# Issue order of the token load and the zero fill at the start of a decoder kernel

## The chip, the core and the metric

The kernel runs on one core of one Trainium2 chip. The time is the device time of one execution in microseconds (us), given as the median of three runs. Besides it there is one profiled execution, whose span runs from the first to the last instruction.

The core has a matrix engine (PE), a vector engine (DVE), an activation engine (ACT), a general one (POOL), and SP, which here does nothing but issue the direct transfers. All of SP's transfers go into one queue that 16 DMA engines serve.

## The reference, cut to what matters

```python
x = x + _L0_attn_ref(_layernorm(x), ...)              # 16 heads, rotary positions
x = x + _L0_xattn_ref(_layernorm(x), itok, ctx, ctx, ctx)  # 4 experts, chosen by token id
x = x + _L0_ffn_ref(_layernorm(x), ...)               # two linears with sign weights
x = x + _L1_attn_ref(_layernorm(x), ...)
x = x + _L1_xattn_ref(_layernorm(x), ctx, mask, ...)
x = x + _L1_ffn_ref(_layernorm(x), ...)
```

`x` is 4 batches of 512 tokens of 512 numbers in float32 (4 MiB). The expert stage takes each token through the one expert that its id picks.

## The kernel before

The whole of `x` stays on the chip in the tile `x`, as 16 tiles of 128 tokens. Seven phases run one after the other with a barrier of all engines between them: `Start`, `Attention` (attn0), `Experts`, `BitMlp`, `Attention` twice more (attn1, xattn) and `Fp8Linear`. Only the first two are touched.

**Start** loads the constants and the tokens, normalises batch 0 into `xn`, and works out on DVE to which row of a sorted list each token belongs (`place`). The sorted list, `sorted_x`, is a tensor in DRAM of 19 slots of 128 rows; each expert's part is padded up to whole slots. So that the padding holds zeros, all of `sorted_x` is first filled from `zero`, the last 512 columns of `arena` (L263, semaphore `filled`, of which the later phase knows `m.zero_filled`). `x` is loaded in two pieces (L259): batch 0 with the semaphore `x_loaded[0]`, then batches 1 to 3 with `x_loaded[1]`, known later as `m.x_all`. Between the two, `sp_following` issues the first two weight matrices of attn0 (keys and queries).

**attn0** begins on SP with seven loads of constants (L552: biases, `rope_cos`, `rope_sin`, `rope_rot`), then `weights.sp_rest`: the value weights and the output weights (L356), each as soon as the buffer it reuses has been split into its two float16 halves (ACT L372, then DVE L376; `weight_low` counts those). Then SP waits for the constants and enters a loop over the batches. In it, SP issues 48 small copies (L568) that stack the projected keys and queries into `kst` and `qst`; the first 12 wait for two finished projections (`fl`, counted by POOL at L1064), the next 12 for four, then six, then eight. Behind them come the copies of the row maxima (L573).

The projections of one batch go so: PE makes projection `n` (12 matmuls, L389), ACT reads it with its bias into `qb` (L790), POOL multiplies by the cosines (L1025, `t1`), PE turns it by a matmul with `rot` (L651), DVE multiplies by the sines (L926), adds both (L930) and rounds (L932), POOL takes the low half (L1064). `qb` and `t1` have two buffers: ACT may read projection `n` only when `t1` of `n - 1` is there, so with no work from POOL two projections are read and no third. Then PE makes the values, mixed with the row maxima's matmuls (L599), of which the first waits for the first 24 stacking copies (`stacked[0]`).

POOL's part of attn0 (the function `pool`) begins with a memset (L1010), waits for the constants, and then, before it enters the loop over the batches, for the zero fill:

```python
if self.rope:
    g.wait_ge(*m.zero_filled)
with g.Fori(0, NB) as b:
```

This is there since POOL scatters the tokens into `sorted_x` at the end of every batch. `m.x_all` is waited for later: by POOL behind the projections of a batch, by DVE at its fourth unit of the heads.

Of the kernel before, what the change touches and what calls it, by code (L numbers as in the profile page):

```python
# [12 lines left out]
P = 128  # L13
NB = 4
# [4 lines left out]
T = S // P  # L19
# [30 lines left out]
class Chain:  # L50


    def __init__(self, phase, sem, per, b):
        self.at, self.sem, self.per, self.base, self.n = phase.at, sem, per, b * per, 0
# [12 lines left out]
class Machine:  # L67
# [53 lines left out]
    def take(self, n, dt=F32):  # L121

        words = (n + 1) // 2 if dt == F16 else n
        a = self.arena[:, self.used:self.used + words]
        self.used += words
        assert self.used <= ARENA, self.used
        return a if dt == F32 else a.bitcast(dt)
# [70 lines left out]
class Phase:  # L198
# [16 lines left out]
    def sp_following(self, sp):  # L215
        if self.following:
            self.following.sp_early(sp)

    def sp_early(self, sp): pass
# [5 lines left out]
    def sp(self, sp): pass  # L225


class Start(Phase):
# [7 lines left out]
    def __init__(self, m):  # L236
        super().__init__(m, "start")
        s, take = self.sem, m.take
        self.x_loaded, self.const = self.sems("x_loaded", 2, 16), s("const_loaded", 16 * 4)
        self.norm = Norm(m, "norm", 1)  # L240
        self.consts, self.memsets, self.filled = s("consts_done", 2), s("ones_and_zero", 2), s("zero_filled", 16)
        n = NE * NB * T
        e_t = lambda a: a.rearrange("p (e t) -> p e t", e=NE)
        self.ids = take(NB * T, I32)
        self.own, self.total, self.before, self.rank = (e_t(take(n)) for _ in range(4))
        self.tri, self.ones, self.starts = take(P), take(P), take(NSLOT)
        self.cut = e_t(take(n))
        self.n, self.tiles, self.base = take(NE), take(NE), take(NE)
        self.placef, self.expertf = take(NB * T), take(NSLOT)
        self.zero = m.arena[:, ARENA - D:]  # L250
        self.own_made, self.counted, self.chain = s("experts_known", 1), s("tokens_counted", 1), s("chain", 60)
        m.zero_filled, m.x_all = self.at(self.filled, 16), self.at(self.x_loaded[1], 16)

    def sp(self, sp):
        m, io = self.m, self.io
        for dst, src in ((self.ids, io["itok_cols"]), (m.ident[:], io["ident"]), (self.tri, io["triangle"]), (self.starts, io["slot_starts"])):
            sp.dma_start(dst, src).then_inc(self.const, 16)
        for k, b in ((0, slice(0, 1)), (1, slice(1, NB))):
            sp.dma_start(m.x[:, b.start * T:b.stop * T, :], io["x"][b].rearrange("b (t p) d -> p (b t) d", p=P)).then_inc(self.x_loaded[k], 16)  # L259
            if k == 0:  # L260
                self.sp_following(sp)
        sp.wait_ge(*self.at(self.memsets, 2))
        sp.dma_start(io["sorted_x"].rearrange("(s p) d -> p s d", p=P),  # L263
                     self.zero.rearrange("p (a d) -> p a d", a=1).broadcast_to([P, NSLOT, D])).then_inc(self.filled, 16)

    def pool(self, g):
# [127 lines left out]
class Attention(Phase):  # L394
# [118 lines left out]
    def row(self, g, j):  # L513
        n = self.ROWS * g + j
        return n % 2, n // 2
# [23 lines left out]
    def sp(self, sp):  # L539
        m, io = self.m, self.io  # L540
        row = lambda a: a.rearrange("(a n) -> a n", a=1).broadcast_to([P, D])
        loads = [(self.vb, row(self.v_bias)), (self.ob, row(self.out_bias)),
                 (self.pb[:, 0:C], self.biases[0]),
                 (self.pb[:, C:2 * C], self.biases[1])]
        if self.rope:
            loads += [(self.cos, io["rope_cos"]), (self.sin, io["rope_sin"]), (self.rot, io["rope_rot"])]
        if self.cross:
            loads += [(self.gamma, row(io["L1_xattn_ln_gamma"])), (self.beta, row(io["L1_xattn_ln_beta"])),
                      (self.rs, io["L1_xattn_residual_scale"].rearrange("(a n) -> a n", a=1).broadcast_to([P, 1])),
                      (self.mask, io["mask_cols"])]  # L550
        for dst, src in loads:
            sp.dma_start(dst, src).then_inc(self.const, 16)  # L552
        self.weights.sp_rest(sp)
        sp.wait_ge(*self.at(self.const, 16 * len(loads)))

        with sp.Fori(0, NB) as b:
            if self.cross:
                nb = (b + 1) % NB
                sp.wait_ge(*self.at(self.audio_low, b + 1))
                sp.dma_start(m.raw[:, 0],  # L560
                             io["ctxT"][bass.ds(nb * D, D), :].rearrange("(c p) o -> p c o", p=P)).then_inc(self.audio_loaded, 16)
            for half in range(2):
                order = ((0, self.kst, (0, 0, 1)), (1, self.qst, (0, 1, 0)))
                for n, (w, stack, parts) in enumerate(reversed(order) if self.cross else order):
                    sp.wait_ge(*self.at(self.fl, b * self.NPROJ + 4 * half + 2 * (n + 1)))
                    for r, part in enumerate(parts):
                        for j in range(HG):
                            sp.dma_start(stack[HD * r:HD * (r + 1)].rearrange("p (c j) t -> p c j t", j=HG)[:, 2 * half:2 * half + 2, j, :],  # L568
                                         self.qf[HD * j:HD * (j + 1), w, part, 2 * half:2 * half + 2]).then_inc(self.stacked[half], 16)
            if not self.cross:  # L570
                for g in range(C):
                    self.row_wait(sp, self.row_free, self.row(g, self.ROWS - 1), b, 1)
                    sp.dma_start(self.qst[3 * HD:3 * HD + 1, HG * g:HG * (g + 1), :].rearrange("p h t -> p (h t)"),  # L573
                                 self.mt[0:HG * T, :]).then_inc(self.mdma, 16)
        if self.cross:
            sp.wait_ge(*self.at(self.audio_low, NB + 1))
        else:
            self.weights.wait(sp, len(self.weights.mats) - 1)
        if self.rope:
            for k in range(2):  # L580
                sp.wait_ge(*self.at(self.row_free[k], T // 2 + NB * (self.row_items // 2)))
        self.sp_following(sp)
        if self.rope:
            self.following.weights.sp_rest(sp)
# [1258 lines left out]
```

## Time and profile before

| | us |
|---|---|
| median of 3 runs | 2064.85 |
| lowest, highest | 2061.89, 2064.95 |
| span of the profiled execution | 2056.5 |
| median less this span | 8.35 |

The profiled execution has no time of its own beside its span; the 8.35 us between the span and the median are taken as what lies around it. The page of the profile gives shares of busy time over the whole span; for a change in the first 100 us of 2056.5 us, the list of instructions in order of time is of more use. In it, a bracket behind a row tells how long the engine was idle ahead of the row and what released it, and rows with SPq are transfers as SP issues them: their duration is that of the issue, not of the transfer.

### The profile page before, as it was taken

The numbers are of one execution on the slowest core, as the hardware profiler recorded it, in microseconds if no ns is written. First come the engines' busy times: TensorE is split into PE (matmuls) and PEld (weight loads), VectorE is DVE, ScalarE is ACT, GpSimd is POOL, SyncE is SP. The second block draws the span as 40 slices with busy tenths as digits, with TensorE's granted clock in tenths as the row PEclk, the third lists the DMA queues.
The fourth block names the chain that finished last, engine by engine and source line by source line (L and its number), as shares of the span: only waits on it lengthen the run. The fifth ranks groups of instructions, "written<-read, shape, count | busy, mean of one in ns | idle before, by whom it ended". The sixth has DMA issues, their size and how long they took to land.

```text
span 2056.5 us, 28429 instructions
## 1 busy us (share of the span) xinstructions
PE 1639.2 (80%) x9252; PEld 640.5 (31%) x9253; DVE 1369.1 (67%) x2092; ACT 854.3 (42%) x1015; POOL 522.9 (25%) x413
## 2 busy tenths in 40 slices
PE   1998898988948935777699899999697887877837
PEld 1323233232336622333323333232232312222213
DVE  3876867858645537999285564738547677666868
ACT  1152240532523315776435353534546262542613
POOL 1514216133120015111401212130232311313117
PEclk9999999999979977998899999999899999898968
DMA  7201103002124444000210202020330110202102
GB/s 284 63 2 36 46 0 80 2 22 60 42 91 143 143 128 62 1 0 0 80 34 3 60 0 61 0 51 10 123 82 21 33 28 20 61 20 51 31 5 82
DMA packets 80843, 106.08 MB, mean 52 GB/s; under 512 B 14112, under 2 KB 51360, under 8 KB 80672
## 3 DMA queue, kind: packets, MB, share of 16 engines
q1 hardware_dynamic: 77216, 97.14, 15.9%
q0 software_dynamic: 3584, 8.39, 2.0%
q8 instruction: 24, 0.39, 0.1%
q14 instruction: 19, 0.16, 0.0%
HBM read 49.26 MB, written 18.35 MB: 33 GB/s over the span
## 4 chain that ended last, share of the span: by engine, by line
PE 35%; issue 25%; DVE 19%; POOL 6%; SPq 5%; ACT 4%; DMA 3%; DVEq 1%; POOLq 0%; ACTq 0%
PE ps L389 13%; PE ps L630 11%; SPq L568 5%; DVE arena L825 5%; PE ps L599 5%; PE ps L729 4%; DVE arena L970 2%; DVE arena L845 2%; POOL arena L1064 2%; DVE stats L171 1%; ACT arena L806 1%; DVE arena L1486 1%; DMA arena<-arena 1%; DVE arena L1497 1%; PE ps L615 1%
## 5 line engine op out<-in xcount | busy, mean ns | idle before, releaser
L630 PE MATMUL ps<-arena 128*32 128x512 f32 x3072 | 399.5, 623 | 45.1 <-ACT arena L806 33.0
L825 DVE TENSOR_REDUCE arena<-ps 128x1 f32<-128x512 f32 x512 | 323.1, 678 | 147.3 <-PE ps L599 146.9
L806 ACT ACTIVATE arena<-ps 128x1024 f32<-128x1024 f32 x256 | 252.1, 1025 | 314.9 <-PE ps L729 313.8
L389 PE MATMUL ps<-xt,w 128*128 128x512 f16 (+1 forms) x1872 | 293.4, 310 | 36.1 <-DVE arena L876 17.9
L729 PE MATMUL ps<-arena 97*128 97x512 f16 (+1 forms) x768 | 216.8, 386 | 19.2 <-DVE arena L970 15.1
L599 PE MATMUL ps<-arena 96*128 96x512 f16 x512 | 186.8, 398 | 53.1 <-DMA arena<-arena 33.9
L389 PEld LDWEIGHTS ps<-xt,w 128*128 128x128 f16 (+1 forms) x1872 | 156.9, 100 | 176.3 <-issue 66.2
L389 PE MATMUL ps<-w,arena 128*128 128x512 f16 (+1 forms) x804 | 180.0, 381 | 12.7 <-issue 12.7
L806 ACT ACTIVATE arena<-arena 128x1024 f32<-128x1024 f32 x128 | 134.0, 1056 | 130.9 <-DVE arena L970 125.1
L970 DVE TENSOR_SCALAR arena<-ps,arena 128x1024 f32<-128x1024 f32 x128 | 157.1, 1256 | 38.4 <-PE ps L729 38.1
L1004 POOL TENSOR_TENSOR arena<-arena 128x512 f32<-128x512 f32 x36 | 57.2, 1589 | 447.3 <-DVE arena L845 447.3
L790 ACT ACTIVATE arena<-ps,arena 128x512 f32<-128x512 f32 x96 | 65.8, 686 | 250.8 <-PE ps L389 127.0
L630 PEld LDWEIGHTS ps<-arena 128*32 128x32 f32 x3072 | 78.1, 111 | 218.5 <-issue 187.4
L1064 POOL TENSOR_TENSOR arena<-arena 128x512 f16<-128x512 f32 x96 | 111.6, 1163 | 133.8 <-ACT arena L794 112.9
L845 DVE RECIPROCAL arena<-arena 128x128 f32<-128x128 f32 x144 | 132.4, 933 | 0.0
L599 PEld LDWEIGHTS ps<-arena 96*128 96x128 f16 x512 | 45.2, 98 | 250.9 <-DVE arena L825 178.4
L192 POOL TENSOR_TENSOR rstd<-mv,eps 128x4 f32<-128x4 f32 x30 | 6.5, 215 | 451.3 <-DVE mv L175 451.3
L838 DVE TENSOR_TENSOR xt<-ps,xt 128x512 f16<-128x512 f32 x60 | 40.6, 682 | 115.2 <-ACT xt L744 115.2
L389 PEld LDWEIGHTS ps<-w,arena 128*128 128x128 f16 x804 | 77.9, 98 | 114.6 <-issue 23.5
L389 PE MATMUL ps<-w,xt 128*128 128x512 f16 x384 | 111.1, 408 | 0.0
L729 PEld LDWEIGHTS ps<-arena 97*128 97x128 f16 (+1 forms) x768 | 68.5, 99 | 129.0 <-issue 51.1
L171 DVE BATCH_NORM_STATS2 stats<-x 128x6 f32 (+1 forms) x104 | 64.2, 680 | 22.4 <-DMA x<-sorted_y,place 16.7
(171 smaller groups left out, 2089.0 us busy)
## 6 DMA issues: line engine op xcount, KB each, us to landing
arena<-arena SPq DMA_DIRECT2D x576, 64.0 KB, 2.0
raw<-in_ctxT SPq DMA_DIRECT2D x8, 1024.0 KB, 5.4
raw<-in_ffn_parts SPq DMA_DIRECT2D x16, 512.0 KB, 3.5
sorted_x<-arena SPq DMA_DIRECT2D x1, 4864.0 KB, 29.4
arena<-sorted_x SPq DMA_DIRECT2D x19, 256.0 KB, 3.5
sorted_y<-arena SPq DMA_DIRECT2D x19, 256.0 KB, 2.1
out<-x SPq DMA_DIRECT2D x16, 256.0 KB, 2.1
x<-in_x SPq DMA_DIRECT2D x1, 3072.0 KB, 17.4
```

Source lines behind the costliest of these rows:

```text
L171: v.bn_stats(m.stats[:, i, :], src(i)).then_inc(self.sums, 1)
L389: last = pe.matmul(out, left[l](cl[k]), right[r](cr[k]), start=start and k == 0 and a == 0, stop=stop and k == n - 1 and a == 2)
L568: sp.dma_start(stack[HD * r:HD * (r + 1)].rearrange("p (c j) t -> p c j t", j=HG)[:, 2 * half:2 * half + 2, j, :], self.qf[HD * j:HD * (j ...
L599: pe.matmul(self.row_bank(at), self.qst[0:3 * HD, head, t * P:(t + 1) * P], self.kst[0:3 * HD, head, :], start=True, stop=True).then_inc(s ...
L630: last = pe.matmul(self.m.ps[HD * j:HD * (j + 1), 7 if ones else 6, :], left, self.pt[:, u % 2, j * S:(j + 1) * S], start=kb == 0, stop=kb ...
L729: last = pe.matmul(self.m.ps[:, j4, :], self.kst[0:R, HG * g + j4, kb * P:(kb + 1) * P], self.qst[0:R, HG * g + j4, :], start=True, stop=True)
L790: act.activation(self.qb[:, n % 2, :], self.bank(item), ACT.Identity, scale=s, bias=self.pb[:, C * w + c:C * w + c + 1]).then_inc(self.ban ...
L806: act.activation(out, src, ACT.Exp, scale=SOFTMAX_SCALE).then_inc(self.exp_done[h], 1)
L825: v.tensor_reduce(self.mx[:, j:j + 1], self.row_bank(at), AX.X, ALU.max).then_inc(self.row_free[at[0]], 1)
L845: v.reciprocal(part, part).then_inc(self.inverted, 1)
L970: v.tensor_scalar(self.pt[:, u % 2, 2 * h * S:(2 * h + 2) * S], flat(m.ps[:, 2 * h:2 * h + 2, :]), slot_col(self.hi, b * T + kb), -50.0 / ...
L1064: g.tensor_tensor(self.qf[:, w, 1, c, :], src[:, n % 2, :], self.qf[:, w, 0, c, :], ALU.subtract).then_inc(self.fl, 1)
```

## The change

The load of batches 1 to 3 and the zero fill are taken out of `Start.sp` and put into a function `sp_late`, which attn0 calls on SP behind its constants and the rest of its weights, ahead of the wait for the constants. The wait on the memsets ahead of the fill goes, since a barrier now lies between. No other engine's program changes; POOL still waits for the zero fill ahead of its loop.

```diff
         m.zero_filled, m.x_all = self.at(self.filled, 16), self.at(self.x_loaded[1], 16)
+        m.start_late = self.sp_late
...
-        for k, b in ((0, slice(0, 1)), (1, slice(1, NB))):
-            sp.dma_start(m.x[:, b.start * T:b.stop * T, :], io["x"][b].rearrange("b (t p) d -> p (b t) d", p=P)).then_inc(self.x_loaded[k], 16)
-            if k == 0:
-                self.sp_following(sp)
-        sp.wait_ge(*self.at(self.memsets, 2))
-        sp.dma_start(io["sorted_x"].rearrange("(s p) d -> p s d", p=P),
+        self.load_x(sp, slice(0, 1), self.x_loaded[0])
+        self.sp_following(sp)
+
+    def load_x(self, sp, b, loaded):
+        sp.dma_start(self.m.x[:, b.start * T:b.stop * T, :], self.io["x"][b].rearrange("b (t p) d -> p (b t) d", p=P)).then_inc(loaded, 16)
+
+    def sp_late(self, sp):
+
+        self.load_x(sp, slice(1, NB), self.x_loaded[1])
+        sp.dma_start(self.io["sorted_x"].rearrange("(s p) d -> p s d", p=P),
                      self.zero.rearrange("p (a d) -> p a d", a=1).broadcast_to([P, NSLOT, D])).then_inc(self.filled, 16)
...
         self.weights.sp_rest(sp)
+        if self.rope:
+            m.start_late(sp)
         sp.wait_ge(*self.at(self.const, 16 * len(loads)))
```

SP's queue before, from the query weights of attn0 on (the end of `Start` and the head of attn0; `in_L_attn_v_wT` are the value weights, `in_L_attn_out_wT` the output weights, `phase_end` is the barrier):

```order
L356 DMA raw<-in_L_attn_q_wT 128x4x512
L259 DMA x<-in_x 128x12x512
L263 DMA sorted_x<-arena 128x19x512 [waits ones_and_zero]
L552 DMA arena<-in_L_attn_v_b 128x512 [waits phase_end]
L552 DMA arena<-in_L_attn_out_b 128x512
L552 DMA arena<-in_L_attn_k_b_cols 128x4
L552 DMA arena<-in_L_attn_q_b_cols 128x4
L552 DMA arena<-in_rope_cos 128x512
L552 DMA arena<-in_rope_sin 128x512
L552 DMA arena<-in_rope_rot 128x128
L356 DMA raw<-in_L_attn_v_wT 128x4x512 [waits weight_low]
L356 DMA raw<-in_L_attn_out_wT 128x4x512 [waits weight_low]
```

The same place in the changed kernel, whose line numbers are up to 7 higher:

```order
L361 DMA raw<-in_L_attn_q_wT 128x4x512
L557 DMA arena<-in_L_attn_v_b 128x512 [waits phase_end]
L557 DMA arena<-in_L_attn_out_b 128x512
L557 DMA arena<-in_L_attn_k_b_cols 128x4
L557 DMA arena<-in_L_attn_q_b_cols 128x4
L557 DMA arena<-in_rope_cos 128x512
L557 DMA arena<-in_rope_sin 128x512
L557 DMA arena<-in_rope_rot 128x128
L361 DMA raw<-in_L_attn_v_wT 128x4x512 [waits weight_low]
L361 DMA raw<-in_L_attn_out_wT 128x4x512 [waits weight_low]
L263 DMA x<-in_x 128x12x512
L268 DMA sorted_x<-arena 128x19x512
```

The two large transfers have moved behind nine others, and behind the two waits on `weight_low`.

POOL in the changed kernel, at the head of attn0 (a memset, the branch into the loop with its waits, the first products with the cosines):

```order
L1017 MEMSET arena 1x8192 [waits phase_end]
L1024 UNCONDITIONAL_BRANCH [waits zero_filled,consts_done,const_loaded]
L1024 ISA
L503 ISA [waits norm_xn_ready]
L1031 ISA [waits bank_free0]
L1032 TENSOR_TENSOR arena<-arena 128x512 [waits rotated]
L1032 TENSOR_TENSOR arena<-arena 128x512 [waits rotated,bank_free1]
```

Nothing moved here: these rows stand in the same order before, with line numbers lower by 7.

## Rows read from the trace of the kernel before

**Rows 1.** The page: the chain that ended last, share of the span by engine.
```profile
PE 35%; issue 25%; DVE 19%; POOL 6%; SPq 5%; ACT 4%; DMA 3%; DVEq 1%; POOLq 0%; ACTq 0%
```

**Rows 2.** Timeline of SP: start, us, what it issues, count.
```profile
12.59 0.51 SPq L356 DMA_DIRECT2D raw<-in_L_attn_q_wT  x1
13.14 0.73 SPq L259 DMA_DIRECT2D x<-in_x  x1
13.92 5.65 SPq L263 DMA_DIRECT2D sorted_x<-arena  x1
29.90 4.85 SPq L552 DMA_DIRECT2D arena<-in_L_attn_v_b  x1
...
40.55 0.38 SPq L356 DMA_DIRECT2D raw<-in_L_attn_v_wT  x1
42.75 0.38 SPq L356 DMA_DIRECT2D raw<-in_L_attn_out_wT  x1
64.81 31.90 SPq L568 DMA_DIRECT2D arena<-arena  x48
```

**Rows 3.** DMA, 0 to 80 us: GB/s by 2 us; issues: count, KB, us to landing.
```profile
GB/s 0 0 0 4 0 64 143 346 389 403 395 344 400 400 385 410 410 404 410 408 383 292 318 406 393 212 6 0 0 0 0 0 0 107 71 107 108 97 107 100
...
sorted_x<-arena SPq DMA_DIRECT2D x1, 4864.0 KB, 29.4
x<-in_x SPq DMA_DIRECT2D x1, 3072.0 KB, 17.4
...
x<-in_x SPq DMA_DIRECT2D x1, 1024.0 KB, 5.5
...
raw<-in_L_attn_q_wT SPq DMA_DIRECT2D x1, 1024.0 KB, 9.8
```

**Rows 4.** Stages: PE, PEld, DVE, ACT, POOL busy, granted PE clock, DMA share, GB/s.
```profile
15.00:50.00 35.00, 6.12 (x22) 3.88 (x22) 17.45 (x52) 7.16 (x7) 8.19 (x3) 1.00 1.04 384
...
82.30:86.00 3.70, 3.67 (x10) 1.35 (x11) 2.07 (x4) 0.00 (x0) 3.52 (x3) 0.54 0.43 104
```

**Rows 5.** Timeline of ACT, DVE and PE, 38 to 60 us.
```profile
38.23 4.49 DVE L376 SCALAR_TENSOR_TENSOR w<-raw,w 128x2048 f16<-128x2048 f32 x2 [1.11 <-ACT w L372]
47.90 7.25 PE L389 MATMUL ps<-xt,w 128*128 128x512 f16 x24 [12.14 <-DMA arena<-in_rope_rot]
52.76 1.91 ACT L372 ACTIVATE w<-raw 128x2048 f16<-128x2048 f32 x1 [0.66 <-DMA raw<-in_L_attn_out_wT]
54.70 2.29 DVE L376 SCALAR_TENSOR_TENSOR w<-raw,w 128x2048 f16<-128x2048 f32 x1 [0.28 <-ACT w L372]
59.71 2.75 PE L389 MATMUL ps<-xt,w 128*128 128x512 f16 x12
```

**Rows 6.** Timeline of POOL, 55 to 84 us.
```profile
55.42 3.92 POOL L1025 TENSOR_TENSOR arena<-arena 128x512 f32<-128x512 f32 x2 [18.57 <-ACT arena L790]
60.44 1.16 POOL L1064 TENSOR_TENSOR arena<-arena 128x512 f16<-128x512 f32 x1 [1.09 <-DVE arena L932]
61.55 1.72 POOL L1025 TENSOR_TENSOR arena<-arena 128x512 f32<-128x512 f32 x1
63.63 1.16 POOL L1064 TENSOR_TENSOR arena<-arena 128x512 f16<-128x512 f32 x1 [0.36 <-DVE arena L932]
...
67.93 1.72 POOL L1025 TENSOR_TENSOR arena<-arena 128x512 f32<-128x512 f32 x1
...
76.77 1.16 POOL L1064 TENSOR_TENSOR arena<-arena 128x512 f16<-128x512 f32 x1 [0.36 <-DVE arena L932]
...
83.59 4.93 POOL L1035 TENSOR_TENSOR x<-x,arena 128x512 f32 x4
```

**Rows 7.** The chain that ended last, 38 to 100 us: start, us, what.
```profile
54.58 0.68 ACT arena L790
...
58.09 1.26 POOL arena L1025
...
82.33 0.90 PE ps L599 x2
```

## The prediction

> **What bounds the kernel now.** I read the page first. PE leads the chain that ended last with 35% of the span; DMA has 3% of it [rows 1]. So transfers bound no long stage, and whatever this change does, it does in the first 100 us, where the page has no detail. There I read the timeline of SP beside the landing times, then the timelines of the engines that wait for what lands, and last the chain of that stretch, to see which wait ends last.
>
> The landing times, added to the issues, put the queries' weights at 12.59 + 9.8 = 22.4, the rest of `x` at 13.14 + 17.4 = 30.5 and the fill at 13.92 + 29.4 = 43.3 [rows 2, 3]. They land one behind the other: the 3 MiB of `x` 8.1 us behind the weights (2.7 us for each MiB), the 4.75 MiB of the fill 12.8 us behind `x`. The queue carries 384 GB/s on average for as long as it has work [rows 4]. Attn0's constants are issued at 29.90 and stand behind the fill. PE has been idle for 12.14 us when `rope_rot` releases it at 47.90 [rows 5].
>
> The chain shows that PE's start is not yet the last wait. It goes through the output weights (issued at 42.75, releasing ACT at 52.76), ACT's split of them [rows 2, 5], ACT's first reading of a projection at 54.58, POOL's product with the cosines, and from 64.81 through SP's 48 stacking copies, to PE's first row maximum at 82.33 [rows 7]. From 64.81 on SP itself is the pace: 48 issues take 31.90 us, with no room between them [rows 2].
>
> **What the change takes away.** The constants meet an empty queue at 29.90 (the queries' weights landed at 22.4), so they land in the middle thirties. PE may then start when the keys' weights are split. DVE makes two splits from 38.23 in 4.49 us, so the first is there at 40.5 [rows 5]. PE's start moves from 47.90 to about 40.6, 7.3 us earlier. The value weights are issued at 40.55 as before, since they wait for that split and not for the constants, and now land at 40.55 + 5.5 = 46.0, as batch 0 (the 1 MiB of `x`) did from an empty queue; the output weights at about 48.5. ACT splits the last in 1.91 us, to 50.4, and reads the first projection at 50.4 in place of 54.58 (4.2 us earlier), and DVE has made its last split by 52.7, where it made it from 54.70 on [rows 2, 3, 5, 7].
>
> **What it adds.** POOL waits for the fill ahead of its loop. Before, that wait cost nothing: the fill landed at 43.3, and POOL's first product began at 55.42, released by ACT [rows 6]. Now the fill stands behind the value weights, the output weights and 3 MiB of `x`. SP issues the output weights at 42.75, the load at 43.2 and the fill at 43.9. I add the measured steps between landings: output weights 48.5, `x` + 8.1 = 56.6, fill + 12.8 = 69.4 [rows 2, 3]. The other way: 1 + 1 + 3 + 4.75 MiB are 10.22 million bytes, which at 384 GB/s take 26.6 us; the first MiB from an empty queue took 5.5 - 2.7 = 2.8 us over its pace, which bounds the time until data flows [rows 3, 4]. From 40.55 that gives 70.0 at the latest; at 410 GB/s, the best of the single slices [rows 3], 24.9 us and 1.8 us of start give 67.2, the earliest. I take **69.2**, next to the sum of the steps.
>
> What is queued behind the wait: POOL's products with the cosines. ACT reads two projections and no third, PE makes four projections and two turns and then stops, DVE makes one product with the sines and stops. SP's first stacking copy waits for the second low half. All of attn0 stands on that POOL wait. The two items that go and come are not added: what is won until 50.4 vanishes in a wait that ends at 69.2.
>
> **From the fill to the path.** Before, the first product ran from 55.42 to 58.09, 2.67 us, while DVE split the last weights (54.70 to 56.99); the next took 1.26 us [rows 5 to 7]. Now DVE stands still then, so the first takes 1.26 as well: it ends at 69.2 + 1.26 = 70.5 where it ended at 58.09, **12.4 us later**. From the end of the first product to the end of the second low half there are 6.7 us before (58.09 to 63.63 + 1.16 = 64.79) [rows 6, 7]. Every idle piece of POOL in this stretch is ended by DVE's L932, not by PE or ACT [rows 6]; so PE's lead of two projections shortens nothing here, and I carry the 6.7 over whole. Bound below: POOL's four operations alone, 1.26 + 1.16 + 1.26 + 1.16 = 4.8, which would give back 1.9 us. So SP starts stacking at 64.81 + 12.4 = 77.2.
>
> From there the 48 issues at 31.90 us set the pace as before; the later groups of twelve wait for projections that POOL finishes at its old pace of 3.2 us each (products at 61.55 and, two later, 67.93 [rows 6]), and POOL's lead on SP there stays. PE's first row maximum comes at 82.33 + 12.4 = 94.7, and nothing behind it has slack that could swallow this: the chain runs on from it through PE and DVE. The load of `x`, at 56.6, is first needed by POOL, at 83.59 before [rows 6]: it costs nothing in either kernel. Nor does the issue of the fill on SP (5.65 us, ended by 49.6 [rows 2]), since SP's next work is at 77.2.
>
> The sum: span 2056.5 + 12.4 = 2068.9, and with the 8.35 around it **2077.2 us**, 0.6% more than 2064.85.
>
> The rate of the queue can be held against a rule. The row shows 384 GB/s over 35 us [rows 4]. The Trainium skill, page "DMA: Bandwidth & Descriptors", section Specifications, states a limit of about 358 GB/s from HBM for one core and a ceiling of 435 GB/s of the fabric. By the first, the 10.22 MB would take 28.5 us and the fill land at 71.1, an estimate from that page, for 2079.1 us in all; by the second 23.5 us, 66.1 and 2074.1 us. The trace is above the first figure, so it does not bind here.
>
> **The rivals.**
>
> *A, the fill is not what ends last, and the kernel is faster.* Place: POOL's wait ahead of its loop. If the fill landed before ACT's first reading at 50.4, POOL would begin its products about 4.2 us earlier, at 51.2, and win up to 1.4 us more since DVE's last split lies beside less of the first: 2064.85 - 5.6 = 2059.3 us. It decides at a landing of 56.8: below that the change gains, above it loses. For 56.8 the queue would need 10.22 MB in 14.3 us, 715 GB/s. Load and fill go in different directions (DRAM to chip, chip to DRAM), which speaks for some overlap; but before, the fill ended 12.8 us behind the load, which is its own full time at 390 GB/s, so the two did not overlap [rows 2, 3]. Chance 0.04.
>
> *B, PE's lead is given back.* PE has projections 2 and 3 ready when POOL begins, and the stretch of 6.7 us shrinks towards 4.8, with the fill at 67.2: 12.4 - 1.9 - 2.0 = 8.5, thus 2073.4 us. For it: what PE would still have to make, 12 matmuls in 2.75 us for each projection [rows 5], is done for two of them. Against: SP needs only the first two low halves, and those hang on POOL and DVE. Chance 0.12.
>
> *C, the queue is slower or PE resumes slowly, and it costs more.* PE will be idle from about 58 to 71. After an idle of 12.14 us the 24 matmuls at 47.90 took 7.25 us where 12 later take 2.75 [rows 5]; from 82.3 to 86, where PE resumes after its wait for the stacking copies, the granted clock was 0.54, near the lower of its two levels, 1.2 GHz [rows 4]. Cold, projection 4 takes 5.1 in place of 2.75 us: ACT's third reading ends 0.8 us after the first product, turn 2.0, projection 5.1, ACT 0.7, in all 8.7 us; POOL needs it after 67.93 - 58.09 = 9.8 [rows 6, 7]. So 1.1 us are left, and behind that SP's queue hides another 2 us for its third group (the sixth low half is there at 76.77 + 1.16 = 77.9, and SP needs it after half of its 31.90 us, at 80.7 [rows 2, 6]). If both covers failed, 2.4 us: 2079.6; with the fill at 70.0, 2080.4 us. Chance 0.14. The Trainium skill, page "TensorE: Matmul & The Clock Gate", section "HAM oscillation — how this bites in real kernels", warns of matrix work that starts cold after every long wait; here that would be one start, not many, and rows above price it.
>
> *D, no change in effect.* Batch 0's delay would be swallowed before the end of attn0, by a later wait on something that isn't delayed: 2064.9 us. Against: the chain goes through SP's copies and PE's row maxima without a break [rows 2, 7], and no transfer of that stretch runs by a time of its own. Chance 0.03.
>
> **How the numbers follow.** My forecast, 2077.2 with bounds of the landing (67.2 to 70.0) 2075.2 to 2078.0, has 0.67, B 0.12, C 0.14, D 0.03, A 0.04. The three runs of before spread over 3 us, of which about 1.5 may lie between any two medians. The range takes in B and C with that: **2072 to 2081.5**. It leaves out A, D and the far ends of B and C, together less than 2 in 10. A measurement can tell about 0.2% (4.1 us) from no change: slower than that are the forecast and C whole and nearly all of B, 0.93; within it D and a piece of A, 0.04; faster 0.03.
>
> **What would show it.** In the profile of the changed kernel: PE's first projection near 40.6; constants landed before 37; the value weights landed near 46 and the output weights near 48.5; POOL's first cosine product near 69.2, released by the fill's transfer after some 32 us of idle, and 1.26 us long; SP's first stacking copy near 77.2; PE's first row maximum near 94.7; behind that everything 12.4 us later, with a span near 2069. POOL's first product before 56.8 would mean A; between 60 and 67 a queue faster than I take it; a first stacking copy less than 8 us behind POOL's first product B; an issue gap in SP's 48 copies C.

## The result: 0.6% slower, held by POOL's wait for the fill

| | before | changed | |
|---|---|---|---|
| median of 9 runs each, us | 2064.06 | 2075.27 | +11.2 |
| lowest to highest, us | 2056.9 to 2070.0 | 2072.2 to 2080.6 | |
| ratio | | 1.0061 | 95% interval 1.0048 to 1.0074 |
| span of the profiled execution, us | 2056.5 | 2073.2 | +16.7 |

The forecast was 2077.2 us (2072 to 2081.5); the median is 2075.27. By the ratio the change costs 12.6 us (9.9 to 15.3), 2064 us being the time of before; the prediction added 12.4 us. Where a ratio is turned into us below, it is done in this way.

SP's timeline of the changed kernel (start, us of the issue, what) answers to [rows 2]. The first constant is issued in 0.34 us, where it took 4.85, and the two large transfers stand last:

```profile
29.96 0.34 SPq L557 DMA_DIRECT2D arena<-in_L_attn_v_b  x1
...
32.72 0.43 SPq L557 DMA_DIRECT2D arena<-in_rope_rot  x1
40.62 0.38 SPq L361 DMA_DIRECT2D raw<-in_L_attn_v_wT  x1
42.82 0.38 SPq L361 DMA_DIRECT2D raw<-in_L_attn_out_wT  x1
43.24 0.51 SPq L263 DMA_DIRECT2D x<-in_x  x1
43.79 5.56 SPq L268 DMA_DIRECT2D sorted_x<-arena  x1
78.74 31.31 SPq L575 DMA_DIRECT2D arena<-arena  x48
```

The landings, from the list of DMA issues of the first 90 us (count, KB, us from issue to landing), beside [rows 3]:

```profile
sorted_x<-arena SPq DMA_DIRECT2D x1, 4864.0 KB, 26.5
x<-in_x SPq DMA_DIRECT2D x1, 3072.0 KB, 15.0
...
raw<-in_L_attn_v_wT SPq DMA_DIRECT2D x1, 1024.0 KB, 5.2
raw<-in_L_attn_out_wT SPq DMA_DIRECT2D x1, 1024.0 KB, 7.2
...
arena<-in_rope_rot SPq DMA_DIRECT2D x1, 64.0 KB, 4.2
```

So the last constant is there at 36.9 (47.5 before), the output weights at 50.0, the load of `x` at 58.2 and the fill at 70.3. PE, ACT and POOL, from the timelines, beside [rows 5] and [rows 6]:

```profile
40.84 6.65 PE L394 MATMUL ps<-xt,w 128*128 128x512 f16 x24 [5.00 <-DVE w L381]
...
72.92 2.04 PE L658 MATMUL ps<-arena 128*128 128x512 f32 x2 [10.95 <-ACT arena L797]
74.76 4.18 PE L394 MATMUL ps<-xt,w 128*128 128x512 f16 x12
```

```profile
50.00 1.91 ACT L377 ACTIVATE w<-raw 128x2048 f16<-128x2048 f32 x1 [2.22 <-DMA raw<-in_L_attn_out_wT]
51.82 1.25 ACT L797 ACTIVATE arena<-ps,arena 128x512 f32<-128x512 f32 x2
72.09 0.69 ACT L797 ACTIVATE arena<-ps,arena 128x512 f32<-128x512 f32 x1 [19.02 <-POOL arena L1032]
```

```profile
70.79 2.49 POOL L1032 TENSOR_TENSOR arena<-arena 128x512 f32<-128x512 f32 x2 [33.87 <-DMA sorted_x<-arena]
```

PE starts 7.1 us earlier, released by DVE and no longer by a constant, and ACT reads the first two projections 2.8 us earlier. Then ACT stands for 19.02 us until POOL has made a product, and POOL stands for 33.87 us until the fill has landed. Before, ACT was what released POOL. ACT's third reading starts at 72.09, as POOL's first product ends (72.01): with projections counted from 0, reading `n` waits for `t1` of `n - 2`, not of `n - 1` as the section on the kernel before has it; that two readings and no third go without POOL is right.

The chain that ended last, 38 to 110 us (start, us, what), beside [rows 7]:

```profile
43.79 26.48 DMA sorted_x<-arena
70.90 1.11 issue
72.01 1.27 POOL arena L1032
...
78.74 0.76 SPq L575
...
93.68 1.99 DMA arena<-arena
95.71 1.03 PE ps L606 x2
```

The fill itself now lies on the chain, with its whole 26.48 us. PE's first row maximum comes at 95.71, 13.4 us later than before.

### The profile page after: what moved, and what is told of

The parts are those of the page before. It is cut to its first block, busy times and chain, and to the rows that moved or that the text cites. A ratio compares the mean times of both kernels' runs of the same rounds, so it can differ in the third digit from the quotient of the medians.

```text
span 2073.2 us, 28429 instructions
## 1 busy us (share of the span) xinstructions
PE 1647.8 (79%) x9252; PEld 642.5 (31%) x9253; DVE 1371.2 (66%) x2092; ACT 854.5 (41%) x1015; POOL 521.7 (25%) x413
## 3 DMA queue, kind: packets, MB, share of 16 engines
q1 hardware_dynamic: 77216, 97.14, 15.9%
## 4 chain that ended last, share of the span: by engine, by line
PE 36%; issue 25%; DVE 19%; SPq 5%; POOL 5%; ACT 4%; DMA 4%; DVEq 1%; POOLq 0%; ACTq 0%
PE ps L394 12%; PE ps L637 11%; SPq L575 5%; DVE arena L832 5%; PE ps L606 5%; PE ps L736 4%; DVE arena L977 2%; DVE arena L852 2%; POOL arena L1071 2%; DVE stats L171 1%; ACT arena L813 1%; DMA sorted_x<-arena 1%; PE ps L1380 1%; DVE arena L1493 1%; DMA arena<-arena 1%
## 5 line engine op out<-in xcount | busy, mean ns | idle before, releaser
L736 PE MATMUL ps<-arena 97*128 97x512 f16 (+1 forms) x768 | 217.8, 387 | 20.2 <-DVE arena L977 16.5
L845 DVE TENSOR_TENSOR xt<-ps,xt 128x512 f16<-128x512 f32 x60 | 40.6, 683 | 115.5 <-ACT xt L751 115.5
```

The lines of the kernel that those rows point to most:

```text
L736: last = pe.matmul(self.m.ps[:, j4, :], self.kst[0:R, HG * g + j4, kb * P:(kb + 1) * P], self.qst[0:R, HG * g + j4, :], start=True, stop=True)
```

## The experiments

Each ratio is taken against runs of the kernel before on the same chip. The profiles come from more than one chip, and the row "before" of the table is the one profile of before shown so far. In the kernels that move POOL's wait, it stands right ahead of the scatter in each batch:

```diff
-        if self.rope:
-            g.wait_ge(*m.zero_filled)
         with g.Fori(0, NB) as b:
...
                 g.wait_ge(*self.at(self.place_ready, b + 1))
+                g.wait_ge(*m.zero_filled)
```

The table has what decides, in the order of PE's first row maximum. Three columns are from the profiled execution: when POOL made its first product, when SP issued the first stacking copy, when PE made its first row maximum. The last is the ratio in us.

| kernel | POOL | SP | PE | PE less before | ratio (interval) | ratio in us |
|---|---|---|---|---|---|---|
| four weights early, wait at scatter | 47.36 | 57.02 | 75.30 | -7.0 | 0.9960 (0.9946 to 0.9975) | -8.3 |
| only x late, after a landing | 52.30 | 62.06 | 80.31 | -2.0 | 0.9975 (0.9963 to 0.9987) | -5.2 |
| only x late | 52.93 | 62.59 | 80.41 | -1.9 | 0.9983 (0.9972 to 0.9994) | -3.5 |
| change, wait at scatter | 51.81 | 61.20 | 82.10 | -0.2 | 0.9999 (0.9986 to 1.0012) | -0.2 |
| before | 55.42 | 64.81 | 82.33 | 0 | 1 | 0 |
| before, wait at scatter | 56.80 | 66.19 | 83.91 | +1.6 | 1.0010 (0.9993 to 1.0026) | +2.1 |
| four weights early, wait at loop | 59.07 | 67.02 | 84.00 | +1.7 | 1.0006 (0.9991 to 1.0020) | +1.2 |
| four weights early, old order | 59.55 | 69.00 | 86.80 | +4.5 | 1.0008 (0.9996 to 1.0021) | +1.7 |
| fill ahead of the rest of weights | 59.36 | 69.03 | 87.00 | +4.7 | 1.0014 (0.9999 to 1.0029) | +2.9 |
| only fill late | 64.12 | 72.08 | 89.08 | +6.8 | 1.0041 (1.0024 to 1.0059) | +8.5 |
| change, fill ahead of x | 64.24 | 72.18 | 89.17 | +6.8 | 1.0032 (1.0016 to 1.0048) | +6.6 |
| the change | 70.79 | 78.74 | 95.71 | +13.4 | 1.0061 (1.0048 to 1.0074) | +12.6 |

The two columns of differences ("PE less before" and "ratio in us") follow each other to within 3.3 us, over a spread of 21. So most of a kernel's gain or loss is there when PE makes its first row maximum; what follows is why that moves. Differences of 2 to 3 us in this table are not told apart.

### POOL's wait moved to the scatter

> The change as it stands, but POOL's wait for the zero fill moved from ahead of its loop to just ahead of the scatter of each batch. Theory (the fill's landing holds POOL, and that is the whole cost): POOL's first cosine product near 52.6 in place of 70.8, SP's first stacking copy near 60, PE's first row maximum between 77 and 81; ratio to before 0.997 to 0.999, some 3 to 5 us faster. Rival (the late traffic itself costs, by holding SP's copies behind 8 MB in the same queue): stacking copies issued from about 60 land only after the fill, near 70.3, and SP's issues beside the fill take up to 1.0 in place of 0.6 us, as the constants did before; the first row maximum then comes at 82 or later and the ratio is 1.000 or more.

Neither theory had it all. POOL was released by ACT again and made its first product 3.6 us earlier than before:

```profile
51.81 3.93 POOL L1030 TENSOR_TENSOR arena<-arena 128x512 f32<-128x512 f32 x2 [14.86 <-ACT arena L797]
```

SP issued its first copy at 61.20. So the 13 us of the change hang on the place of this wait. But the 3.6 us did not arrive: the first row maximum came at 82.10 and the ratio is 0.9999. SP's chain shows where they went (start, us, what):

```profile
61.20 0.76 SPq L575
...
62.00 1.18 SPq L575
...
63.23 1.28 SPq L575
...
64.56 1.31 SPq L575
...
65.90 1.72 SPq L575
...
67.67 0.61 SPq L575
```

Four of the copies take 1.18 to 1.72 us to issue in place of 0.60, while the fill is in the queue (it landed at 43.82 + 25.6 = 69.4); another, at 69.60 and so behind the landing, takes 1.38. One such copy stands in the kernel before too, with no large transfer in the queue:

```profile
68.17 1.10 SPq L568
```

The four cost 3.1 us together. The first copies also took up to 8.0 us to land, where 2.0 is usual, so they landed about when the fill did; but the chain goes through the issues. The 24 copies from the first issue to the last landing took 20.9 us, before 17.5. That is the rival's mechanism, at a price of 3.4 us.

### The two halves of the change

```diff
 # only x late: in Start.sp, behind the first weights
+        sp.wait_ge(*self.at(self.memsets, 2))
+        sp.dma_start(self.io["sorted_x"]..., self.zero...).then_inc(self.filled, 16)
...
 # only fill late: in Start.sp, behind the first weights
+        self.load_x(sp, slice(1, NB), self.x_loaded[1])
```

Each has the same transfer taken out of `sp_late`.

> Only the load of batches 1 to 3 goes behind attn0's weights; the zero fill is issued in the start phase, right behind the first two weights. Theory: fill landed at 22.4 + 12.8 = 35.2, constants by 39, PE's first projection at 40.9, output weights near 48.5, POOL's first product near 51 to 52, ratio 0.997 to 0.999. Rival (the moved load delays what is behind it): PE or POOL released by a transfer later than before, ratio 1.000 or more.

As the theory had it, with POOL 1 us later than its range: the output weights landed at 50.27, not at 48.5. The load landed at 43.39 + 14.9 = 58.3, long before anybody waits for it, so moving it is free here, and it lets the constants and the weights through: 3.5 us faster.

> Only the zero fill goes behind attn0's weights; batches 1 to 3 are loaded in the start phase as before. Theory: fill lands near 50.0 + 12.8 = 62.5, POOL's first product near 62.9, so 62.9 - 55.42 - 1.4 = 6 us later than before on the path; ratio 1.002 to 1.004, about half of the change's own 1.0061. Rival (the cost is having the fill beside attn0 at all, not when it lands): ratio as of the whole change, 1.005 to 1.007.

POOL's timeline:

```profile
64.12 2.49 POOL L1032 TENSOR_TENSOR arena<-arena 128x512 f32<-128x512 f32 x2 [27.07 <-DMA sorted_x<-arena]
```

The fill landed at 43.37 + 20.2 = 63.6, POOL began 8.7 us later than before, and the kernel is 8.5 us slower (5 to 12). The ratio, 1.0041, is just above the range expected (1.002 to 1.004), and its interval reaches into the rival's (1.005 to 1.007); what speaks against the rival is the profile, where POOL waits for the fill and begins 6.7 us earlier than in the change.

### The fill ahead of the load

```diff
     def sp_late(self, sp):
-        self.load_x(sp, slice(1, NB), self.x_loaded[1])
         sp.dma_start(self.io["sorted_x"]..., self.zero...).then_inc(self.filled, 16)
+        self.load_x(sp, slice(1, NB), self.x_loaded[1])
```

> Both moved as in the change, but the fill is issued ahead of the load of batches 1 to 3. Theory: only the fill's landing counts, so as when the fill alone is late: fill near 62.5, POOL near 62.9, ratio 1.002 to 1.004, though the queue carries all 8.1 MB until about 70.3. Rival (what counts is how long the queue is busy beside attn0): ratio 1.005 to 1.007, as the change.

```profile
64.24 2.48 POOL L1032 TENSOR_TENSOR arena<-arena 128x512 f32<-128x512 f32 x2 [27.26 <-DMA sorted_x<-arena]
```

POOL began at 64.24, as with the fill alone, though the load behind it kept the queue busy until 43.85 + 27.8 = 71.7. So it is not the traffic beside the projections that costs, but what POOL waits for. (The load landed before the first copy, at 72.18; this run says nothing of traffic beside the copies, which is what cost 3.4 us above.) In the ratio this kernel is not told apart from the one with the fill alone (1.0032 against 1.0041), and it is 6 us faster than the change, from which it differs only by which of two transfers is issued first.

### The wait in the kernel before

The edit is the one shown above, in the kernel before.

> The kernel before with one edit: POOL's wait for the zero fill moved to just ahead of each scatter. Control. Theory (before the change this wait was over long before POOL could start, at 43.3 against 55.42): nothing changes, POOL's first product near 55.4, ratio 0.9985 to 1.0015. Rival (the place of the wait has a cost of its own): ratio beyond that.

The ratio is 1.0010 (0.9993 to 1.0026): the wait cost nothing where it stood, as expected. The profile shows something else: POOL began at 56.80, in place of 55.42, as the output weights landed at 54.1 and not 52.8, and at 40.99 SP was already 0.44 us later than before, as it was at the first constant (30.34 for 29.90). None of this comes from the edit, which touches only a wait of POOL. Two executions of nearly the same work differ by 1.4 to 1.6 us in this stretch alone; whether that is the execution or the chip, no run tells.

### The fill between the constants and the other weights

```diff
         for dst, src in loads:
             sp.dma_start(dst, src).then_inc(self.const, 16)
+        if self.rope:
+            m.start_fill(sp)
         self.weights.sp_rest(sp)
         if self.rope:
             m.start_late(sp)
```

`start_fill` issues the fill, `start_late` only the load.

> The fill goes behind the constants but ahead of the value and output weights, the load of batches 1 to 3 behind all of them; POOL's wait as in the change. The fill lands 5 us later than before and is still ahead of POOL. Theory (only a landing later than about 56 costs): fill near 33.2 + 2 + 12.8 = 48, value weights near 50.5, output weights near 53.5 as before, POOL's first product near 55 to 56.5, ratio 0.999 to 1.002. Rival (every us by which the fill is moved costs): 5 us, ratio 1.0025.

The fill landed at 34.13 + 15.9 = 50.0, later than before by 6.7 us, and did not hold POOL. This row of ACT shows what did:

```profile
56.70 1.91 ACT L380 ACTIVATE w<-raw 128x2048 f16<-128x2048 f32 x1 [0.80 <-DMA raw<-in_L_attn_out_wT]
```

The output weights, behind the fill in the queue, came at 56.7 in place of 52.8, so POOL began at 59.36, 3 us later than the theory had it: the value weights came 4.0 us behind the fill (54.0) and not 2.5. The ratio, 1.0014 (0.9999 to 1.0029), fits both the theory and the rival (1.0025). By the profile, the 2.9 us (0 to 6) are those of the weights; whether a fill that lands just below 56 is free was not shown by this run.

### A version meant to beat both

```diff
         self.pt = take(2 * HG * S).rearrange("p (n t) -> p n t", n=2)
+        if rope:
+            self.weights.bufs = m.raws + [self.pt[:, k, :].rearrange("p (c o) -> p c o", c=C) for k in range(2)]
...
-                ... t["L0_attn_out_wT"]], m.raws * 2, 2,
+                ... t["L0_attn_out_wT"]], m.raws * 2, 4,
```

On top of the change with POOL's wait at the scatter: the last two weight matrices no longer reuse the first two's buffers, so they need not wait for the splits and are issued in `Start`.

> A version meant to beat both. POOL waits for the fill only ahead of the scatter, and attn0's value and output weights are loaded early too, into the probabilities' buffers (pt), which are free until the heads; batches 1 to 3 and the fill behind the constants as in the change. Theory (what ends last before POOL is ACT's split of the output weights, held by their landing): weights there by 28, ACT splits all four from 36.4 to 43.8, ACT's first reading near 46, POOL's first product near 46, stacking copies from about 54, at most a few of them held by the fill that lands near 56, first row maximum near 72 to 74 in place of 82.3; ratio 0.994 to 0.997. Rival (copies held by the late traffic give most of it back, as with the wait moved alone): first row maximum at 78 or later, ratio 0.998 or more.

It is the fastest kernel of this study: 0.9960 (0.9946 to 0.9975), median 2055.70 against 2063.97 us. ACT splits all four from 36.51 on:

```profile
36.51 3.70 ACT L377 ACTIVATE w<-raw 128x2048 f16<-128x2048 f32 x2
40.11 3.70 ACT L377 ACTIVATE w<-arena 128x2048 f16<-128x2048 f32 x2
46.49 0.69 ACT L799 ACTIVATE arena<-ps,arena 128x512 f32<-128x512 f32 x1 [2.68 <-PE ps L394]
```

What ends last before POOL is now PE's first projection. The first copies are issued at 57.02 and the fill lands at 34.08 + 25.3 = 59.4, so few of them meet it: the 48 took 32.69 us, 0.8 more than before. The stages came 1 to 3 us later than expected, as POOL's first product was at 47.36 and not 46, and the second waited for a projection.

> The kernel before, with attn0's value and output weights loaded early into the same free buffers, but the load of batches 1 to 3 and the fill where they were, ahead of the constants. Theory (one queue in order): load lands near 36, fill near 48.8, the last constant near 52 to 53, so PE's first projection near 53 in place of 47.9 and POOL's first product near 58; ratio 1.000 to 1.002. Rival (early weights alone are the gain of that version, the order of load and fill doesn't matter): ratio 0.997 or less.

Nearly as expected: with the weights early and the old order, the constants stand behind everything, PE starts at 53.87 (released by `rope_rot`), POOL at 59.55 (1.5 us later than forecast, released by ACT, the fill having landed at 49.5), and nothing is won; the ratio, 1.0008, doesn't differ from 1. So the early weights do not pay by themselves. Whether the order of the change is enough for them to pay, the next run asks.

> The faster version (four weights early, load and fill behind the constants) with POOL's wait for the fill put back ahead of its loop. Theory (POOL's wait is the whole difference between the change's order being a gain and a loss): fill lands near 59.4, POOL's first product near 59.9 in place of 47.4, 12.5 us later, ratio near 0.996 + 0.006 = 1.002. Rival (POOL catches up, since PE, ACT and DVE have run ahead): ratio 0.999 or less.

```profile
59.07 2.48 POOL L1034 TENSOR_TENSOR arena<-arena 128x512 f32<-128x512 f32 x2 [22.12 <-DMA sorted_x<-arena]
```

The fill landed at 33.71 + 24.8 = 58.5. The one wait put back, POOL begins 11.7 us later, SP's copies 10.0 and the first row maximum 8.7 us later; in the ratios it is 9.5 us. So a part of the delay, 1.7 us between POOL and SP, is given back here: POOL's second product does not wait for a projection any more (the two take 2.48 us together, where without the wait they begin 2.5 us apart). That is rival B of the prediction, where PE's lead has a use. Between SP and PE another 1.3 us come back, since no copy meets the fill now (the 48 take 31.34 us, 32.69 without the wait). The ratio, 1.0006 (0.9991 to 1.0020), lies between the theory's 1.002 and the rival's 0.999, but its interval is clear of that of the version without the wait (0.9946 to 0.9975). It is also that of the old order with early weights (1.0008): it takes both, the order of the change and the wait at the scatter, for the early weights to pay. (Moving the wait with the old order was not run; there the fill landed 10 us before POOL could begin.)

### The load after the landing of the weights

```diff
         self.weights.sp_rest(sp)
         if self.rope:
+            sp.wait_ge(*self.at(self.weights.loaded[3], 16))
             m.start_late(sp)
```

This stands on top of the kernel with only `x` late.

> As with only the load of batches 1 to 3 moved (fill in the start phase), but SP issues that load only once the output weights have landed. Question: why the output weights, from a queue empty but for the value weights, landed 3.5 to 5.4 us behind those in four kernels and 2.6 behind in the kernel before. Theory (what is issued right behind them shares the engines and holds them): output weights land 5.5 us after their issue near 43, so near 48.5 in place of 50.2, POOL's first product near 51.2 in place of 52.9, the load at 58 to 59, still ahead of the stacking copies near 61; ratio 0.997 to 0.999. Rival (they land late whatever follows): landing near 50, POOL near 53, ratio as before that edit, 0.9983.

Inconclusive. The output weights landed at 49.63, between the 48.5 of the theory and the 50 of the rival, 0.6 us earlier than without the wait (50.27). The ratio, 0.9975 (0.9963 to 0.9987), overlaps that of the kernel without it. Why these weights, behind one transfer alone, land 3.3 us or more behind it and not 2.7 stays open.

## Why the prediction was right, step by step

- **PE's start.** Forecast 40.6, measured 40.84, released by DVE's split of the keys' weights. The constants came by 36.9, as forecast (before 37).
- **The weights.** The value weights were forecast at 46.0 and came at 45.8. The output weights were forecast at 48.5 and came at 50.0: this term was 1.5 us too small. It was taken from one transfer in an idle queue and one step between two landings in a full one; this was neither. ACT's first reading, forecast at 50.4, came at 51.82 by it, which changed nothing, since the fill ended last.
- **The fill's landing.** Forecast 69.2, measured 70.3, just outside the bounds of 67.2 to 70.0. The output weights' 1.5 us came in, the step to the load was right (8.2 us, 8.1 forecast), and the step to the fill gave 0.8 us back (12.0, 12.8 forecast). From 42 to 68 us the queue carried 376 GB/s, again above the 358 GB/s that the Trainium skill, page "DMA: Bandwidth & Descriptors", section Specifications, gives for a core; by that figure the fill would have landed at 71.1, an estimate from that page, which is nearer to 70.3 than the 69.2 is, but for the wrong reason: the rate was higher, and the weights were late.
- **From the landing to POOL.** Taken as nothing; 0.5 us passed (70.3 to 70.79). The first product took 1.22 us (70.79 to 72.01), 1.26 forecast.
- **From POOL to SP.** The 6.7 us that were carried over from the end of the first product to the first copy are 72.01 to 78.74, so 6.7. Rival B, the lead of two projections given back, did not come in the change. The sign that the prediction set for it, a first copy less than 8 us behind POOL's first product, was met by a hair (78.74 - 70.79 = 7.95), but that sign could not tell B from the forecast, which itself stood at 77.2 - 69.2 = 8.0. What tells the two apart is the stretch of 6.7, which B would have made shorter. B was real only where the second product had waited for PE (the version with the early weights).
- **SP's pace.** 31.31 us for the 48 copies (31.90 before). Most of the difference is the one copy of before that took 1.10 us to issue in place of 0.60, at 68.17 (shown above); there is none such here. It is among the first 24, so that 13.9 us of delay at SP's first copy were 13.4 at the first row maximum.
- **Rival C, PE cold.** The rows of PE show it, milder than forecast: the turn at 72.92 took 2.04 us (2.0 forecast) and projection 4 took 4.18 (5.1 forecast), where 12 matmuls took 2.75 when warm. ACT read it at 79.11, and POOL needed it at 81.86. The forecast lead was 1.1 us and the real one 2.1: nothing was lost. The granted clock in that stretch was 0.61, between the lower of its levels, 1.2 GHz, and the full 2.4, and then full (PE, PEld, DVE, ACT, POOL busy, granted clock, DMA share, GB/s):

```profile
72.90:79.00 6.10, 6.08 (x15) 2.47 (x16) 5.65 (x7) 0.69 (x1) 4.65 (x5) 0.61 0.01 3
79.00:90.00 11.00, 11.00 (x44) 4.67 (x42) 10.29 (x11) 2.60 (x4) 9.88 (x7) 1.00 0.38 93
```

- **Rival A** fell with the landing at 70.3, and with the swap of the two transfers: load and fill land one behind the other, 12.0 us apart. **Rival D** fell too: nothing swallowed the delay. At the fourth unit of batch 0's heads POOL's first step of a norm stood at 114.69 before; the same and the last one of its kind (1977.50 before) now:

```profile
129.16 0.20 POOL L192 TENSOR_TENSOR rstd<-mv,eps 128x4 f32<-128x4 f32 x1 [27.37 <-DVE mv L175]
...
1993.82 0.20 POOL L192 TENSOR_TENSOR rstd<-mv,eps 128x4 f32<-128x4 f32 x1 [14.70 <-DVE mv L175]
```

They are 14.5 and 16.3 us later than before. The first 14.5 are the cost as this pair of profiles has it; the delay reached 19 us near 1625 and fell again. The granted clock goes with it, as in this stretch of the changed kernel, which took 111.2 us at 0.96 before:

```profile
1511.10:1624.90 113.80, 98.89 (x539) 34.08 (x538) 67.37 (x73) 55.78 (x66) 26.87 (x23) 0.94 0.18 47
```

- **A step that was wrong and cost nothing.** The prediction read the 8.35 us between the span of before and the median as what lies around a span. The profiled execution of the change has its own time, 2074.96 us, and a span of 2073.2: 1.8 us lie around it, as (1.7 to 1.9) in every run of the experiments, those of the kernel before among them. So the profiled execution of before was most likely one of about 2058 us, near the lowest of its 9 runs. The sum was made of differences within it, and was added to the median, so the error fell out; but it explains why the spans differ by 16.7 us and the ratio by 12.6. The control with the wait at the scatter shows the same from the other side: its row maximum came 1.6 us later with no cause in its code.

The measured sum of the change's own profile is 78.74 - 64.81 = 13.9 us at SP, against a forecast of 12.4. The ratio, 12.6 (9.9 to 15.3), can't tell them apart. The mechanism was right at each step; that 12.4 and 12.6 lie so near each other is partly luck, since on the path the terms were short by 1.6 us at POOL's first product (1.1 at the landing, 0.5 behind it), with the landing just outside its own bounds.

## What to carry to other kernels

A transfer may be moved behind others only as far as the first wait for it allows, or with that wait moved as well; and moving the wait alone made the change no better than before (0.9999), since the copies then met the fill. Ask for each moved transfer who waits for it and where that wait stands in its engine's program: here it stood ahead of a loop, over 100 us before its need (before, POOL's first product stands at 55.42 and its first scatter at 181.09), and had been free by its early landing alone. Of two moved transfers the one without a near reader paid (3.5 us), and the one with a reader cost 8.5 us by itself and 12.6 us behind the other. In one queue, the small copies behind a large transfer pay as well, in the issue too (3.4 us here). Not run were the early weights with only the load moved, and the fill in a queue other than SP's.

## What had not been expected of the hardware

- SP can take longer to issue while much is in the queue: four copies took 1.18 to 1.72 us beside the fill, where 0.60 is usual; the first constant 4.85 us before the change and 0.34 after it, the others 0.69 to 0.98 and 0.43. The issue of the fill took 5.65 us in the kernel before and 0.51 in the one where only the fill was late and nothing was issued behind it until 72.08; in the swapped kernel it was the load, issued after the fill, that took 11.55 us. So the transfer's own size does not set the time. What is outstanding is not the whole account either: the value weights were issued in 0.38 us at 40.55 before, with the fill in the queue until 43.3, and again at 41.26 in the kernel with the fill ahead of them, which landed at 50.0. And single copies take long with no large transfer outstanding: 1.10 us before, 1.86 (at 67.97) in the last kernel above, whose load had landed at 61.0. The cause stays open.
- The output weights landed 2.6 us behind the value weights when both stood behind a long transfer (before: 50.2 and 52.8), 4.1 with the load behind them in the change (45.9 and 50.0) but 3.5 in the same order with the wait at the scatter (45.7 and 49.1), 5.2 with the fill alone behind them (46.2 and 51.45), 5.4 with fill and load (46.1 and 51.5), 3.3 with nothing behind them (46.36 and 49.63). What follows in a queue may hold what is ahead of it; but with 0.7 us between two kernels of the same order, and 3.3 with nothing behind, the load's part is not shown; only with the fill right behind them do the weights stand out.
- The same stretch differs by 1.4 us between the profiled execution of before and that of its control, whose edit touches only a wait of POOL. One profile can't carry a term below that.
